# First inverse, Gram matrices and two set-up steps in the delta and scan stages of a six-stage decoder

## What is computed

```python
# L0_attn: the delta rule, 16 heads of 32
q, k = silu(x @ Wq.T), silu(x @ Wk.T)          # k is then scaled to unit length per head
v, beta = x @ Wv.T, 2.0 * sigmoid(x @ Wbeta.T)
for t in range(512):                            # per head, S is 32 x 32
    S = S + outer(k[t], beta[t] * (v[t] - k[t] @ S))
    o[t] = q[t] @ S
o = rms_per_head(o * sigmoid(x @ Wg1.T @ Wg2.T)) * g_norm
x = layernorm(x + o @ Wo.T)

# L0_xattn: a selective scan over the context, 512 channels, 16 states
u = silu(conv4(ctx @ in_proj.T) + conv_b)
dt_low, Bm, Cm = split(x_proj @ u, [16, 32])
dt = softplus(dt_proj_w @ dt_low + dt_proj_b)
A = -exp(A_log)
h[t] = h[t-1] * exp(dt[t] * A) + dt[t] * u[t] * Bm[t]
y = (h . Cm + D * u) * silu(x)
x = layernorm(x + y)
```

## Time and profile before

| | before |
|---|---|
| median of 3 runs | 3096.39 us |
| lowest and highest | 3091.23, 3103.2 us |
| the profiled execution | 3089.97 us |
| its span in the trace | 3088.2 us |
| busy: PE, DVE, ACT, POOL | 85%, 62%, 47%, 37% of the span |
| mean granted TensorE clock | 0.922 of full |
| delta stage, about | 0 to 734 us |
| scan stage, about | 734 to 1283 us |

### The profile page before, as it was taken

How to read it: one execution, slowest core, us unless ns; L and a number is a source line. 1 busy time by engine, 2 the same in 40 slices (tenths; PEclk the granted TensorE clock), 3 DMA queues, 4 the chain that set the end, 5 groups by cost and what they waited for, 6 DMA issues and landing times.

```text
span 3088.2 us, 50561 instructions
## 1 busy us (share of the span) xinstructions
PE 2628.3 (85%) x20154; PEld 1431.7 (46%) x20154; DVE 1901.0 (62%) x2978; ACT 1458.1 (47%) x2604; POOL 1148.1 (37%) x1072
## 2 busy tenths in 40 slices
PE   5898989875868776799989888898788999999787
PEld 3665656642323322488745444454433333333243
DVE  4233343434899999756436665666735766667387
ACT  3343333314566565343345362635415666666465
POOL 0444453432778776300052615244232332332000
PEclk8999988987989898899989999899888999999899
DMA  3223232213023140322252324233145554442301
GB/s 100 70 63 90 63 90 53 75 43 144 33 98 109 42 172 14 138 96 84 96 153 86 92 97 134 100 121 132 59 119 113 106 123 112 104 100 66 126 28 41
DMA packets 196766, 284.50 MB, mean 92 GB/s; under 512 B 84388, under 2 KB 86468, under 8 KB 195636
## 3 DMA queue, kind: packets, MB, share of 16 engines
q1 hardware_dynamic: 196532, 281.27, 31.1%
HBM read 192.08 MB, written 63.31 MB: 83 GB/s over the span
## 4 chain that ended last, share of the span: by engine, by line
PE 40%; DVE 10%; issue 4%; ACT 4%; POOL 2%; DMA 2%; SPq 1%; DVEq 0%; ACTq 0%; POOLq 0%
PE ps L236 8%; PE ps L3615 4%; PE ps L3628 4%; PE ps L2055 4%; PE ps L2066 4%; PE ps L3547 3%; PE ps L3564 2%; PE ps L3598 2%; PE ps L2721 1%; PE ps L3552 1%; DVE arena L2984 1%; PE ps L2729 1%; DVE arena L2982 1%; DVE arena L1659 1%; ACT cross L3708 1%
## 5 line engine op out<-in xcount | busy, mean ns | idle before, releaser
L236 PE MATMUL ps<-arena 128*128 128x512 f32 (+3 forms) x1296 | 467.4, 512 | 14.5 <-ACT arena L2821 6.1
L3800 DVE TENSOR_REDUCE cross<-ps 128x1 f32<-128x512 f32 x512 | 327.7, 685 | 175.5 <-PE ps L3598 175.4
L1691 POOL TENSOR_TENSOR arena<-arena 128x1024 f32<-128x1024 f32 x128 | 306.1, 2395 | 121.2 <-DVE arena L1683 121.0
L3708 ACT ACTIVATE cross<-ps 128x512 f32<-128x512 f32 x512 | 276.6, 592 | 156.4 <-PE ps L3615 156.1
L236 PEld LDWEIGHTS ps<-arena 128*128 128x128 f32 (+2 forms) x1296 | 191.5, 153 | 242.6 <-issue 166.3
L1707 PE MATMUL ps<-arena 128*128 128x512 f32 x512 | 271.1, 672 | 38.1 <-POOL arena L1691 37.9
L1683 DVE TENSOR_TENSOR_SCAN arena<-ps,arena 128x1024 f32<-128x1024 f32 x128 | 291.6, 2279 | 9.6 <-ACT ps L1674 9.5
L1674 ACT ACTIVATE ps<-arena 128x511 f32<-128x511 f32 x256 | 165.0, 679 | 155.9 <-DVE arena L1683 155.7
L607 POOL TENSOR_TENSOR arena<-arena 128x31 f32<-128x31 f32 (+15 forms) x217 | 133.5, 615 | 261.1 <-DMA arena<-d_a 244.6
L1707 PEld LDWEIGHTS ps<-arena 128*128 128x128 f32 x512 | 105.6, 215 | 192.9 <-issue 126.2
L3615 PE MATMUL ps<-cross,cross 50*128 50x512 f32 x512 | 156.5, 505 | 31.5 <-ACT cross L3708 22.8
(11 more groups left out here) (359 smaller groups left out, 5147.9 us busy)
## 6 DMA issues: line engine op xcount, KB each, us to landing
arena<-d_bc SPq DMA_DIRECT2D x32, 1024.0 KB, 5.4
cross<-d_parts SPq DMA_DIRECT2D x192, 128.0 KB, 4.5
arena<-d_x SPq DMA_DIRECT2D x16, 1024.0 KB, 5.4
d_parts<-cross SPq DMA_DIRECT2D x32, 512.0 KB, 3.7
d_x<-arena SPq DMA_DIRECT2D x48, 256.0 KB, 2.8
arena<-in_D_wlm SPq DMA_DIRECT2D x12, 1024.0 KB, 6.5
d_signs<-arena SPq DMA_DIRECT2D x32, 256.0 KB, 2.2
arena<-arena SPq DMA_DIRECT2D x64, 128.0 KB, 2.1
```

The lines of the kernel that those rows point to most:

```text
L236: ins = pe.e.matmul(ps[:m, :n], lhsT(k), rhs(k), start=(k == 0), stop=(k == chunks - 1))
L1691: pool.e.tensor_tensor(h, h, s.bc[turn % s.SLOTS][:, 1], ALU.mult).then_inc(*pool.up("scan_hC"))
L3708: act.e.activation(s.E[:, k % 2, j], s.rexp.bank((u, i)), ACT.Exp).then_inc(*s.rexp.empty(act, (u, i)))
L3800: dve.e.tensor_reduce(s.mx[:, u % 2, t, h:h + 1], s.rmax.bank((u, m)), AX.X, ALU.max, negate=True).then_inc(*s.rmax.empty(dve, (u, m)))
```

## The change

Three edits. **(1)** In round -1 the two beta products of pair 0 (`dve_beta_v`) leave their places behind the inverse and stand inside it, at its column steps 2 and 4, between a product and its subtraction. **(2)** In rounds 2, 4 and 6 PE does two output tiles, then the Gram matrices of pair n, then the other two tiles; DVE follows in the same order, and `plan` too. Round 8, which has no new pair, only gets its list in two halves. **(3)** At the seam to the scan, POOL's zeroing of `wdt`, SP's load of `wdt` and ACT's exponential of A move from the `..._before` functions into the `..._front` functions of round 7.

```diff
@@ Delta.plan
             if p >= 1 and even:
-                yield from ((("y", p // 2 - 1, t), "dve") for t in range(T))
+                yield from ((("y", p // 2 - 1, t), "dve") for t in range(2))
...
             if front:
                 yield from ((("A", n, e), "dve") for e in range(2))
+            if p >= 1 and even:
+                yield from ((("y", p // 2 - 1, t), "dve") for t in range(2, T))
@@ Delta.pe_all
             if p >= 1 and p % 2 == 0:
-                s.pe_out(pe, p // 2 - 1)
+                s.pe_out(pe, p // 2 - 1, 0)
...
             if front and p % 2 == 0:
                 for _ in s.pe_gram(pe, n):
                     pass
+            if p >= 1 and p % 2 == 0:
+                s.pe_out(pe, p // 2 - 1, 1)
@@ Delta.pe_out
-        for t in range(T):
+        for t in (2 * h, 2 * h + 1):
@@ Delta.dve_inverse
             e.tensor_tensor(pr, spread(s.t32[:, :a, j], 2, m), spread(s.p32[:, a:, j], 1, a), ALU.mult).then_inc(*dve.up_step(st))
+            if j in (2, 4):
+                s.dve_beta_v(dve, 0, j // 2 - 1)
@@ Delta.dve_all
             if p >= 1 and p % 2 == 0:
-                s.dve_residual(dve, p // 2 - 1)
+                s.dve_residual(dve, p // 2 - 1, 0)
             if front and p % 2 == 0:
                 s.dve_gram(dve, n, 0)
                 s.dve_gram(dve, n, 1)
+            if p >= 1 and p % 2 == 0:
+                s.dve_residual(dve, p // 2 - 1, 1)
...
-                    if p % 2 and i in (4, 6):
+                    if back and p % 2 and i in (4, 6):
                         s.dve_beta_v(dve, n, (i - 4) // 2)
@@ Delta.dve_residual: the moments follow the second half only
@@ Scan
     def sp_before(self, sp):
+        pass
+
+    def sp_front(self, sp, ring):
         s = self
         sp.e.wait_ge(*sp.at_all("scan_wdt_zero"))
         sp.e.dma_start(s.wdt[:s.R, :], s.io["B_dtT"]).then_inc(*sp.up("scan_late", 16))
-
-    def sp_front(self, sp, ring):
...
     def pool_front(self, pool, ring, dead):
         pool.e.wait_ge(*dead)
+        pool.e.memset(s.wdt, 0.0).then_inc(*pool.up("scan_wdt_zero"))
...
     def act_front(self, act, ring):
+        act.e.wait_ge(*act.at_all("scan_weights"))
+        act.e.activation(s.A, s.A, ACT.Exp).then_inc(*act.up("scan_exp_a"))
...
     def pool_before(self, pool):
-        pool.e.memset(s.wdt, 0.0).then_inc(*pool.up("scan_wdt_zero"))
...
     def act_before(self, act):
         act.e.wait_ge(*act.at_all("scan_weights"))
-        act.e.activation(self.A, self.A, ACT.Exp).then_inc(*act.up("scan_exp_a"))
```

More of the change, by code:

```diff
@@ L746, in pe_og, with pe_out @@
             ins.then_inc(*R.fill(pe, ("OT", p, c)))
-    def pe_out(self, pe, b):
+    def pe_out(self, pe, b, h):
         s, R = self, self.ring
         pe.e.wait_ge(*R.at_emptied(pe, ("OT", 2 * b + 1, 1)))
-        for t in range(T):
+        for t in (2 * h, 2 * h + 1):
             pe_project(pe, R, ("y", b, t), lambda k: s.ogT[:, k, t * P:(t + 1) * P], lambda k: s.wo[:, k, :], C)
@@ L1243, in dve_og_scale, with dve_residual @@
         e.tensor_tensor(og, og, spread(s.oss, 3, s.HD), ALU.mult).then_inc(*dve.up("delta_og"))
-    def dve_residual(self, dve, b):
+    def dve_residual(self, dve, b, h):
         s, R = self, self.ring
         x = s.x[:, b % 2]
-        for t in range(T):
+        for t in (2 * h, 2 * h + 1):
             dve.e.wait_ge(*R.at_filled(dve, ("y", b, t)))
@@ L1252, in dve_residual @@
             s.norm.dve_tile(dve, x, t)
-        dve.b = b
-        s.norm.dve_moments(dve)
-        dve.b = 0
+        if h:
+            dve.b = b
+            s.norm.dve_moments(dve)
+            dve.b = 0
 class Scan(Stage):
@@ L1352, in sp_before @@
         sp.e.dma_start(s.wdt[:s.R, :], s.io["B_dtT"]).then_inc(*sp.up("scan_late", 16))
-    def sp_front(self, sp, ring):
-        s = self
         sp.e.wait_ge(*ring.at_emptied(sp, ("xd",)))
```

## The result

| | before | after |
|---|---|---|
| median | 3098.26 us (4 runs) | 3057.94 us (4 runs) |
| lowest and highest | 3091.23, 3103.2 | 3053.33, 3062.25 |
| profiled execution, its span | 3089.97, 3088.2 | 3055.48, 3053.7 |
| mean granted clock | 0.922 | 0.923 |

What follows compares the result with a forecast made beforehand. No busy share was taken to bound the touched first quarter, a chain of hand-overs between engines. Terms 16.0 + 8.4 + 7.6 = 32.0 off the median 3096.39 gave 3064.4 us, range 3054 to 3076.

Steps and rivals of the forecast that it cites:

- Edit 1, -16.0: Round -1: with beta products inside the first inverse, PE transposes K of pair 1 at 80.4 instead of 96.39, 16.0 us earlier.
- Edit 2, -8.4: Gram matrices between output tiles: 7.6 from pair 7's earlier inverse, plus 1.7 from the clock, less 0.9 for a POOL stall.
- In pairs 3 and 5 I cost the same advance at nothing: Rounds 2 and 4: the earlier inverse gains 0, as PE began the triangles of pair 3 without a wait.
- The -7.6 for pair 7: Round 6: Gram products end at 578.6 instead of 586.24, so the inverse lands in DT 7.6 us earlier, at 638.5.
- The clock's -1.7: Triangles of pair 7: after 2.2 us of idleness instead of 9.92 they run nearer the 2.4 GHz level, 1.7 us less.
- POOL's +0.9: Inverse of pair 7 on POOL: it now starts beside DVE's scaling, and one such stall costs 0.9 us.
- The cover of 2.4 for tiles 3 and 4: Tiles 3 and 4 come 1.96 us later on PE; 2.4 of cover remain, without it up to 2 us lost per round.
- Edit 3, -7.6: Seam to the scan: softplus starts at 731.5 instead of 740.42, 8.9 earlier, less a table load of 1.28, so 7.6 us.
- The rivals: Seam or pair 7 gives nothing, 0.17; first inverse gives nothing, 0.04; less than it says, 0.07; slower by the clock, 0.04.
- the bound of 11.6 for edit 2: Upper bound of the Gram reordering's gain: all of PE's 9.92 us wait in round 7 and the clock; lower bound 4.
- the signs of being wrong: PE waits before 72 for anything but ACT; pair 7's wait over 5 us or chain later behind triangles; drive awaits B/C row.
- the rival with two terms failing: Whole change: two of the three terms fail, giving 3084 to 3092 us, within 0.5%; chance 0.07.

Runs made afterwards that it cites:

- the late one of round 4 above: Chain 4 in the run with all three edits, but edit 2 in round 6 only and the first sign load early in rounds 2 and 4: 36.9 us less.
- the early load alone: Kernel before, only SP's first sign load issued ahead of the Gram blocks' write and read back in rounds 2 and 4: ratio 0.9988, 3.7 us less.
- the held load: Kernel before with the new Gram order in rounds 2 and 4 only, first sign load held until DVE's chain step 2: ratio 0.9987, 4.0 us less.

## Why the prediction was right, and where its step failed

- **Edit 1, -16.0: right.** Measured -15.8 (10 to 21). The start of chain 0 is 15.1 earlier in the mean of the profiles (114.3 in the eight with the products behind the inverse, 99.3 in the five with edit 1), and 15.8 earlier if it is counted from the inverse's first operation (66.4 and 50.5), whose own start scatters. The blocks, K and queries of PE came as said, and no idleness over 1.4 stands among them. In the trace of the changed kernel the transposes came 13.45 earlier, not 16.0: 1.45 of that was lost ahead of the edit, and the unit product took 1.4 longer beside POOL's copy, since the 3.40 for squares to transposes was taken from pair 0, where POOL was idle.
- **Edit 2, -8.4: the step that failed** is "In pairs 3 and 5 I cost the same advance at nothing". I asked there whether anyone waited for the inverse, and nobody did. I didn't ask who else stood behind the Gram blocks on SP. The term names "SP's write, read back" as moving and stops at the inverse; behind it on SP's list stand the stores of x, the next x and the first sign load, and behind that, on ACT, the masked queries, and behind these, on PE, blocks and chain. Measured: -16.4 instead of -8.4, -7.2 of it in rounds 2 and 4 (-4.7, -4.6 and +2.1). The new order in these two rounds without round 6 gave 11.8. That the stall comes from the late sign load is shown by its rows, by the order of all profiles by the start of the masked queries, and by its absence where the load alone was moved and came in time (three of four chains, the fourth being the late one of round 4 above); how much of the 7 us it makes in the median is open, since the early load alone gave 3.7 (0 to 8) and leaves the second load late, and the held load didn't bring the stall back.
- *The -7.6 for pair 7* was right: the Gram products moved by 7.6. PE's wait for DT fell from 9.92 to 1.68; in the mean it fell from 10.9 in the eight profiles with the old order in round 6 to 2.7 in the six with the new one. With a mean of -9.1 for the stretch a little more came back than -8.4.
- *The clock's -1.7* did not come in the changed kernel: the triangles took 3.61 after 1.68 of idleness, as the 3.64 after 9.92. There the chain ahead of them had already fallen to the lower level (its last 16 L889 took 1.08, the same 16 L885 0.64 in the kernel before). But it did come in the run with edit 2 alone, where the last 16 took 0.64:

```profile
629.14 1.95 PE L727 MATMUL ps<-arena 128*32 128x128 f32 x64 [1.51 <-DMA arena<-d_t]
```

It came in that one of the six profiles with the new order in round 6, the one with the 53.3; in the other five the triangles took 3.39 to 3.64. In four of those the chain ended at the lower level, and in the fifth, which ended at the higher one, PE had waited 5.09. The forecast looked at the idleness alone and not at the level at which the chain ended. Why the chain ends lower in some executions is open.
- *POOL's +0.9* came as +0.4: from its first product to the inverse's way out it took 41.36 before (637.76 - 596.40) and 41.75 after (603.12 - 561.37), and the write and read back ahead of it were 1.3 shorter. The one stall of 0.9 stands in both kernels, beside DVE's product over 128 x 1024 (1.51 instead of 0.63, after: 1.65 instead of 0.77). The scaling, from 561.32 to 563.29, added 0.3: the five POOL operations that began in it took 1.84 together where they took 1.51 before. The rule of the Trainium skill that I held beside it (SBUF — State Buffer, section Who interferes with whom) lets a DVE instruction that holds both port pairs block GpSimd until that one instruction ends. The scaling is four instructions, so the 1.9 that I made of the rule was read too widely; a block of 1.9 did not come, and a shorter one for each instruction is not excluded.
- *The cover of 2.4 for tiles 3 and 4* was read in round 6, and there it held (+0.2). In round 4 it held too. In round 2 there was none: from the fourth tile to the chain's start it took 11.24 before (259.37 to 270.61) and 10.98 in edit 2 alone (262.22 to 273.20), so the tile's delay went through: +2.1. One cover was read for three rounds.
- **Edit 3, -7.6: right.** 7.68 in the trace, 6.5 (1 to 12) in the runs. The table load took 1.28 and nothing beside it: the drain of 1.38 that the Trainium skill adds (ScalarE: Activation LUTs, section What ACT_TABLE_LOAD costs) does not show, since the exponential starts 0.01 behind the load's end. No row of B and C became the wait. The half of the edit on ACT is worth 0.07 in the trace.
- **The rivals.** None came. The range held the time, but the bound of 11.6 for edit 2 did not hold its 16.4; the other two terms lie within theirs. That the range still held is partly luck: 3057.94 is 4 above its lower end, and the 7 us from rounds 2 and 4 stood in none of its terms; room that was meant for edit 3, the clock and the spread took them in. One of the signs of being wrong did show, a chain that starts later behind its triangles (chain 2, +2.1). And the rival with two terms failing was worked out wrongly: 16.0, 8.4 or 7.6 left alone give 3080 to 3089, not 3084 to 3092.

## What to carry to other kernels

When an operation moves up, follow every queue that it issues into, to the end of that queue's list, and ask at each engine what stands behind the last thing released: edit 2 gained 16.4 where 8.4 were forecast, and a good part of the rest, how much is open, hung on a background load that the forecast did not have. Such background work (a sign piece, a weight of a later stage) is better loaded ahead of a wait than behind it, and not just behind a large load; here that took the stall away, though by itself it gave only 3.7 (0 to 8). And read a cover once for each round in which it is needed, not once for the pattern.

## What was not expected of the hardware

- The load of one sign piece (128 x 512) took 2.4 from SP's issue to ACT's start with nothing issued for almost ten before it, 5.5 just behind the load of x in the kernel before (5.4 to 7.0 in the six profiles with the old order), and 8.1 in one execution.
- In chain 2 of the kernel before PE stood still for 2.13, and the groups behind it ran at the 1.2 GHz level (1.23 for four L865 instead of 0.71), so the stall cost more than its own length. In chain 4, after 2.09, the next two groups still ran at the higher level (0.64 and 0.71) and later ones at the lower (1.22).
- A DVE product over 128 x 1024 took 2.61 while POOL copied the same size in 1.89, and 1.23 alone.
